# A decoder block on one core: in the mixing stage, the product that spreads a unit stands one step later

## The reference, cut to what matters

```
logits = (einsum('tzd,ed->tze', x, phi_w) + phi_b).reshape(t, z, 64, 32)
D = softmax(logits, axis=3)         # gathers tokens into slots
C = softmax(logits, axis=2)         # over the 64 experts: mixes slots back
...                                 # Y_tilde = experts(D^T x)
Y = einsum('tznp,npH->tzH', C, Y_tilde)
x = layernorm(x + Y)
```

## Time and profile before

| | us |
|---|---|
| median of 3 runs | 1675.16 (1673.27 to 1678.43) |
| profiled execution, whole | 1674.83 |
| profiled execution, span | 1672.7 |
| PE busy over the span | 1475.8 (88%) |
| DVE busy | 1229.4 (73%) |
| POOL busy | 1027.9 (61%) |
| ACT busy | 884.0 (53%) |
| a read of kept logits, issue to landing, median | 3.2 |

### The profile page before, as it was taken

How to read it: one execution, slowest core, us unless ns; L and a number is a source line. 1 busy time by engine, 2 the same in 40 slices (tenths; PEclk the granted TensorE clock), 3 DMA queues, 4 the chain that set the end, 5 groups by cost and what they waited for, 6 DMA issues and landing times. The chain is left out here.

```text
span 1672.7 us, 41151 instructions
## 1 busy us (share of the span) xinstructions
PE 1475.8 (88%) x15742; PEld 1181.5 (71%) x15742; DVE 1229.4 (73%) x2454; ACT 884.0 (53%) x1546; POOL 1027.9 (61%) x960
## 2 busy tenths in 40 slices
PE   5664899999999997799999999977999999999997
PEld 4553677777777775577777777756888888888886
DVE  5995577777667775698889888875667777677774
ACT  3774344444343433567777677744555555555554
POOL 3442222332223230699999999974888888888886
PEclk9995799999999998999999999999999999999999
DMA  5111000000000000522222222212222222222220
GB/s 153 32 33 31 5 7 7 7 6 6 7 7 7 6 6 10 156 82 77 80 79 76 82 76 79 79 39 76 73 77 80 73 70 73 71 84 75 70 73 23
DMA packets 47828, 89.99 MB, mean 54 GB/s; under 512 B 5085, under 2 KB 17438, under 8 KB 47650
## 3 DMA queue, kind: packets, MB, share of 16 engines
q1 hardware_dynamic: 46050, 83.07, 14.5%
q0 software_dynamic: 1088, 4.19, 0.8%
q10 hardware_dynamic: 512, 0.23, 0.0%
HBM read 49.73 MB, written 37.75 MB: 52 GB/s over the span
## 5 line engine op out<-in xcount | busy, mean ns | idle before, releaser
L1216 PEld LDWEIGHTS mix_Y<-kept_phi,mix_cT 128*128 128x128 f32 x2048 | 240.1, 192 | 80.2 <-ACT mix_cT L1232 72.4
L1216 PE MATMUL mix_Y<-kept_phi,mix_cT 128*128 128x128 f32 x2048 | 256.8, 279 | 45.0 <-ACT mix_cT L1232 45.0
L1290 POOL TENSOR_TENSOR mix_c<-mix_e,mix_rinv 128x1024 f32<-128x1024 f32 x128 | 243.6, 1903 | 84.3 <-DVE mix_rinv L1282 84.2
L983 POOL TENSOR_TENSOR gather_d<-gather_e,gather_rinv 128x1024 f32<-128x1024 f32 x128 | 246.3, 1924 | 51.8 <-DVE gather_rinv L962 51.4
L1232 ACT COPY mix_cT<-mix_T 128x1024 f32<-128x1024 f32 x128 | 129.8, 1014 | 245.0 <-PE mix_T L1223 245.0
L759 POOL TENSOR_TENSOR cross_veps<-cross_mv,kept_eps 128x1 f32<-128x1 f32 x64 | 12.3, 192 | 342.2 <-DVE cross_mv L706 342.2
L1274 DVE TENSOR_REDUCE mix_sums<-mix_e 128x16 f32<-128x1024 f32 x128 | 155.5, 1215 | 29.1 <-ACT mix_e L1238 25.9
L958 DVE TENSOR_REDUCE gather_rsum<-gather_e 128x32 f32<-128x1024 f32 x128 | 156.0, 1219 | 24.3 <-ACT gather_e L931 24.2
L1257 DVE TENSOR_REDUCE mix_mx<-mix_L 128x16 fp32r<-128x1024 f32 x64 | 78.3, 1224 | 125.9 <-PE mix_L L1200 125.9
L631 ACT ACTIVATE cross_pT<-cross_P,cross_fb 77x1024 f32<-77x1024 f32 x128 | 135.2, 1105 | 65.3 <-PE cross_P L576 65.3
L977 POOL TENSOR_TENSOR gather_dl<-gather_d,gather_dh 128x512 fp32r<-128x512 f32 x128 | 165.9, 1296 | 0.0
(11 more groups left out here) (202 smaller groups left out, 3615.1 us busy)
## 6 DMA issues: line engine op xcount, KB each, us to landing
kept_logits<-gather_keep SPq DMA_DIRECT2D x128, 256.0 KB, 2.0
mix_read<-kept_logits SPq DMA_DIRECT2D x64, 512.0 KB, 3.2
attn_xTg<-in_xT SPq DMA_DIRECT2D x16, 256.0 KB, 2.6
kept_xres<-in_x POOLq DMA_DIRECT2D x4, 1024.0 KB, 11.2
out<-mix_res SPq DMA_DIRECT2D x32, 128.0 KB, 1.8
cross_cg<-in_ctxT SPq DMA_DIRECT2D x32, 58.5 KB, 1.7
setup_wT<-in_w_qkvT SPq DMA_DIRECT2D x1, 192.0 KB
kept_consts<-in_consts SPq DMA_DIRECT2D x1, 68.0 KB
```

The lines of the kernel that those rows point to most:

```text
L983: pool.tensor_tensor(dd[u % 4][:].rearrange("p i (n s) -> p i n s", n=16), e[u % 2][:], rinv[u % 2][:].rearrange("p (i n) -> p i n", i=2). ...
L1216: ins = pe.matmul(psY[t % 2][:, 0:128], cT[u % 2][:, c, :], w.yk[:, 8 * (u % 2) + c, :], start=(u % 2 == 0 and c == 0), stop=(u % 2 == 1 a ...
L1290: pool.tensor_tensor(cc[u % 2][:], e[u % 2][:], rinv[u % 2][:].unsqueeze(2).to_broadcast([128, 16, EXPERTS]), ALU.mult)\
```

## The change: what it does

On PE, Y of a unit stands at lag 4 instead of 3. The result of ACT goes from lag 6 to 7, the residual, the statistics and the mean and variance on DVE from lag 5 to 6, the three small operations on POOL from lag 5 to 6. SP's program is the same; its waits are on counts. The range of steps is one longer.

```
-        ORDER = range(UNITS + 7)
+        ORDER = range(UNITS + 8)
...
# tensor
-                for u in units(k, 3):
+                for u in units(k, 4):
                     t = u // 2
                     pe.wait_ge(cT_ready, u + 1)
...
# scalar
-                for t in tiles(k, 6):
+                for t in tiles(k, 7):
                     act.wait_ge(shift_ready, t + 1)
...
# vector
-                for t in tiles(k, 5):
+                for t in tiles(k, 6):
                     dve.wait_ge(cT_read, 2 * t + 2)
                     reach(dve, res_ready, t - 1)
...
-                for t in tiles(k, 5):
+                for t in tiles(k, 6):
                     dve.wait_ge(st_done, t + 1)
                     dve.memset(w.scratch[:], 0.0)
                     dve.bn_aggr(mv[t % 2][:], stats[:]).then_inc(mv_ready, 1)
...
# gpsimd
-                for t in tiles(k, 5):
+                for t in tiles(k, 6):
                     pool.wait_ge(mv_ready, t + 1)
```

## The result

| kernel | median, us | runs |
|---|---|---|
| before | 1676.80 (1673.27 to 1680.05) | 4 |
| after | 1709.70 (1706.63 to 1711.02) | 4 |

The ratio is 1.0194, with a 95% interval of 1.0167 to 1.0222: the change makes the kernel slower, by 33 us between the medians. The interval lies clear of no change and on both sides of 2%. The forecast was 1712, its range 1700 to 1727. The two profiled executions are 36.0 us apart (1710.85 and 1674.83).

What follows compares the result with a forecast made beforehand. The prediction took the 8.07 us per-tile loop through ACT's copy as the bound; afterwards a one-tile loop of 8.74 us would bind, 60 x 0.66 = +39.6, -3 and +0.4 giving +37 and 1712 us, range 1700 to 1727.

Steps and rivals of the forecast that it cites:

- The loop through the copy: In mixing, PE's groups with ACT's copy mix_cT before Y: a closed loop of 8.07 us per tile, the bound before.
- the loop of one tile: In mixing, from L through DVE, POOL's odd mix_c and T to the next L: 7.23 us before, 8.74 after.
- the added pieces: Residual and statistics on DVE add 0.53 us per tile, mix_mv's wait and three small operations 0.98 on POOL's side.
- The 0.99 per tile: Gain in mixing from removing Y's wait for the copy, if PE's own 7.08 us per tile became the pace.
- The turn of parity: Once-per-tile work on DVE and POOL goes from odd to even steps, lengthening a one-tile loop from 7.23 to 8.74 us.
- The sum: Mixing at 8.74 us per tile: 60 tiles +39.6, first three tiles -3, the end +0.4, in all +37 us.
- The faster one: Rival: mix_mv's wait on POOL is hidden, so mixing runs at 7.75 or 7.08 us per tile, 1655 or 1611; 5%.
- The half one: Rival: in mixing the small operations count, residual and statistics don't; 8.21 us per tile, +5 us, 1680; 4%.
- The clock: Rival: PE's clock falls in the new gap of mixing; +2.1 us per tile where it holds, 1800 throughout; 3%.
- The signs: Expected in mixing's profile: waits near 88 us before T and 116 before mix_veps, last-ending chain through DVE and POOL.
- PE's gap: PE waits 0.67 us before Y every tile; by the skill's rule alone, removing it gives mixing PE's 7.08 us.
- Its estimate: With DVE's recorded durations as gaps, three boundaries each some 0.08 us longer: 8.9 per tile and 1723; not adopted.

Runs made afterwards that it cites:

- e7: Kernel before plus three extra statistics operations per tile on DVE behind mix_mx, results unused; 1692.77 us, ratio 1.0111, 8.34 us per tile.
- e6: Kernel after with DVE's once-per-tile work at lag 7, POOL's three small operations at 8, ACT's result at 9; 1617.47 us, ratio 0.9657.
- e2: Kernel before with only Y moved, from lag 3 to 4; 1692.22 us, ratio 1.0107, 8.38 us per tile.
- e3: Kernel after with Y back at lag 3, so only the once-per-tile work moved; 1715.26 us, ratio 1.0230, 8.67 us per tile.
- e1: Kernel after with the once-per-tile work one lag later again (DVE and POOL 7, ACT 8); 1643.68 us, ratio 0.9829.
- e5: Kernel after with residual and statistics at lag 7, mean and variance and the small operations at 8, ACT's result at 9; 1674.65 us, ratio 1.0003.

## Why the prediction was right, step by step

- **What bounded before.** The loop through the copy was 8.07 and measured 8.08. But the prediction said "The loop is closed, so it is the bound", and stopped. A second loop, over two tiles, was just as long: L to mix_mx 1.66, sums 1.14, odd mix_c 1.58, mix_less 1.86, small operations 1.87, even mix_c 1.15, T 2.05, copy 1.07, Y 1.07, T 1.88, L 0.80, 16.1 us or 8.07 per tile. e7 shows that it was within 0.03 per tile of the pace (0.58 / 2 = 0.29 added, 0.26 seen). It did no harm here, since the copy's wait lies in both loops and a third loop became longer than either.
- **What the change removes.** Y's wait went entirely. Shift to Y was taken at 0.47 by an estimate and is 0.52. PE alone needs about 7.1, and e6 ran at 7.20, which is the loop of one tile without the added pieces: 1.67 + 1.14 + 1.58 + 1.96 + 0.85. The 0.99 per tile that the prediction called "there to be had if nothing else binds" did not come with Y's step alone: e2 was slower than the kernel before.
- **What it moves.** The turn of parity was the cause, and the loop was the one named. e3 shows that it alone gives the new pace, e1 that without it the same Y gains 30 us.
- **The sum.** 8.74 per tile was forecast, 8.68 measured. The terms: mix_c to T 1.96 for 2.05, T to L 0.85 for 0.80, sums to mix_mv 1.13 for 1.15, statistics to sums 0.21 for 0.22, the rest within 0.01. The 2.05 came from a T that stood behind a running Y, and so it measured when PE was done with Y, not the release; on a waiting PE the first transpose starts together with its weight load (both at 1413.79). 60 tiles gave 36.0 us (60 x 0.60) where +39.6 stood. The first three tiles gave -2.1 (-3 forecast; L of the fourth came 21.55 us behind the first L, and 23.65 before), the end +0.7 (+0.4 forecast). Stages ahead of mixing shifted by 1.5 us between the two executions, which the prediction did not foresee and which is no effect of the loop. So the closeness of +37 to the 36.0 between the profiled executions is in part luck, since an error of 3.6 in the loop was made up by that shift and the small terms; between the medians it is 32.9, and the median before had meanwhile moved from 1675.16 to 1676.80 with its fourth run.
- **Rivals.** The faster one (5%) falls: the one-tile loop grew by 1.45 us (7.23 to 8.68), all that the added pieces come to. The half one falls by the period (8.68, not 8.21) and by e5, which has the small operations without residual and statistics and is 0.54 shorter. The clock stayed 1.00, at 1.31 us of PE idle per tile.
- **The signs.** Waits of 77.6 us before T and 111.6 before mix_veps were forecast as 88 and 116. One sign was wrong in form: the chain was to go "through DVE and POOL", and it stays on POOL, as shown above.
- **PE's gap.** In e6 the gap before Y is gone and every other loop is short, and 56 us are gained; in the kernel after the same gap is gone and 33 us are lost. The Trainium skill's "Perfetto Trace Analysis", section Optimization Strategy, says to make what the gap waits for finish sooner; e6 bears that out, and the kernel after shows that here it was not enough.
- **DVE's overlap.** mix_y starts 1.15 behind mix_mx, whose record is 1.23, and the two other boundaries in the loop are 0.08 and 0.07 shorter than the record as well (0.21 for 0.29, 1.13 for 1.20). The Trainium skill's "VectorE: DVE Perf Modes", section The DRAIN you can't avoid, says that the next op does not start until the pipe is empty, and in the same paragraph that a next op that is not held back starts earlier. The prediction used the first sentence alone, and the rows agree with the second. Its estimate is also added up short: three times 0.08 on 8.74 is 9.0 per tile and 1726, not 8.9 and 1723.

## What to carry to other kernels

In a schedule written out in steps, each engine in order, the pace is the longest closed loop of waits divided by the tiles it spans. List them all, with their length, before moving anything: a loop at 7.23 under a pace of 8.07 is slack of 0.84 and no more, and several loops can tie. A lag moved by one changes the parity of work done every second step, and so its neighbours in each queue. Move it by two, or put the small instruction that waits behind a producer from the step before: in e5 and e6 the same three operations stand in the same place of the queue, and the step of their producer alone makes 57 us.

## What the runs showed of the hardware that was not expected

In the kernel after, a group of transposes released from a wait costs PE 0.85 to the next group (0.84 to 0.86 over the tiles), and one behind running products 0.79; but from the start of what it waited for it comes 1.96 behind instead of 2.05. So a row read from a busy PE overstated a wait's price by 0.04 us.
